# Second attention: one DMA transpose per query tile in place of two

## The chip, the cores and the metric

One of the eight cores of a Trainium2 chip runs the whole program. The metric is device time in microseconds (us), the median of some executions. Five engines work side by side, each in the order of its own instruction stream: TensorE (PE, its weight loads PEld), VectorE (DVE), ScalarE (ACT), GpSimd (POOL) and SyncE (SP), which here issues nearly all the DMAs. They meet only at semaphores.

## The reference

Two pre-norm layers over one sequence of 2048 tokens, width 256. Each layer adds an attention and a feed-forward block to the residual. The change touches the attention of the second layer alone:

```python
q = concat([q_c, rope(q_r)]); k = concat([k_c, rope(k_r)])   # 16 heads, 128 + 64 wide
scores = einsum('bqhd,bkhd->bhqk', q, k) / sqrt(128 + 64)     # no mask: 2048 x 2048 per head
probs  = softmax(scores)
ctx    = einsum('bhqk,bkhd->bqhd', probs, v)
x      = x + ctx @ out_w.T + out_b
```

## The kernel before

The second attention is worked off in 256 tiles: 16 heads by 16 tiles of 128 queries (`TILES = NH * NT`). The 2048 keys of a tile n come in two halves g = 0, 1 of 1024. All weights are folded so that keys and values share one 64-wide latent (`kv16`).

For each half: PE writes the scores into one of three score slots (`psS`, L1630 to L1632); DVE takes the row minimum of the negated scores (`half`, L1777 for half 0, L1782 for half 1, whose result is the shift of the whole tile); ACT takes the exponential into `prob` (`exponential`, L1968); ACT writes `prob`, lifted and rounded to fp16, as the high part (`high`, L1978); DVE writes the rest, again fp16, as the low part (`low`, L1790). Both parts of a half stand in `parts[:, s]`, 2 x 1024 columns in a ring of `RING = 4` halves, that is two tiles. Slot s is `(2n + g) % 4`. SP turns a slot by one DMA transpose into `partsT[:, s]`, sixteen blocks of 128 x 128 (`turn_probabilities`, L2164). PE then multiplies the turned blocks with the values (`context`, L1647 and L1648), 32 matmuls a half.

The order on each engine is written out by hand, one step per tile n:

- PE: scores (n+1, 0), scores (n+1, 1), a piece of the next head's projection in 12 of 16 tiles, context (n-2, 0), context (n-2, 1), the output projection of an older tile in every second head.
- DVE: half (n+1, 0), low (n, 0), half (n+1, 1), a rotation in 8 of 16 tiles (L1760), invert (n-2) (L1801), low (n, 1).
- ACT: exponential (n, 0), normalise (n-3), take_output, high (n, 0), exponential (n, 1), a rounding or folding in 8 of 16 tiles, high (n, 1).
- SP: transpose of (n, 0), once in four tiles of every second head the transpose of four tiles' contexts (`turn_contexts`, L2174, 8 blocks), transpose of (n, 1). Some weight loads of the feed-forward block stand between the tiles of the last two heads.
- POOL: small sums and splits, each placed behind a `low_done` count.

Two waits hang on the landing of a transpose. `high` (n, g) overwrites the slot of tile n-2 and waits until that slot's transpose has read it, that is, landed. `context` (n, g) waits for its own. The transpose of (n, g) itself waits for `low` (n, g), and for the context that last read its slot of `partsT` (`pv_done`). Each slot has a landing semaphore of its own. `turns(n, g)` counts how many times the slot of (n, g) has been used.

Of the kernel before, what the change touches and what calls it, by code (L numbers as in the profile page):

```python
# [44 lines left out]
def decoder_two_layers(nc, x_in, wq0, bq0, wk0, bk0, wv, bv, wout, bout, rwT, ewT, eb3, c_pick,  # L45
# [12 lines left out]
    pe, dve, act, pool, sp = nc.tensor, nc.vector, nc.scalar, nc.gpsimd, nc.sync  # L58
    top = ExitStack()

    def sb(ctx, name, shape, dt=F32, side=None):
        return ctx.enter_context(nc.sbuf_tensor(name, shape, dt, side=side))

    def sem(name):
        return top.enter_context(nc.semaphore(name))
# [1075 lines left out]
    def second_attention():  # L1141
# [314 lines left out]
        QS, RING = 5, 4  # L1456
# [7 lines left out]
        parts = sb(L, "parts", [P, RING, 2, HB], F16)  # L1464
        partsT = sb(L, "partsT", [P, RING, 2, HB // P, P], F16)
# [10 lines left out]
        folded, rested = sem("b_folded"), sem("b_rested")  # L1476
        score_ready, half_min, shift_ready, exp_done = sem("b_score"), sem("b_half_min"), sem("b_shift"), sem("b_exp")
        high_done, low_done = sem("b_high"), sem("b_low")
        landed = [sem(f"b_landed{s}") for s in range(RING)]
        pv_done, inverted, ctx_taken, ctx_split = sem("b_pv"), sem("b_inverted"), sem("b_ctx"), sem("b_ctx_split")  # L1480
        ctx_landed = [sem(f"b_ctx_landed{s}") for s in range(2)]
        out_ready, out_taken, out_added = sem("b_out"), sem("b_out_taken"), sem("b_out_added")
# [9 lines left out]
        TILES = NH * NT  # L1492
# [24 lines left out]
        def half_at(n, g):  # L1517

            return (2 * n + g) % RING

        def turns(n, g):

            return (2 * n + g) // RING + 1
# [15 lines left out]
        def outputs(n):  # L1539

            pairs, i = divmod(max(n, 0), 2 * NT)
            return pairs * NT + max(i - NT, 0)

        def has_output(n):
            return 0 <= n < TILES and n // NT % 2 == 1

        def batch(n):

            return (n // (2 * NT)) * (NT // BATCH) + n % NT // BATCH
# [33 lines left out]
        def tensor():  # L1583
# [51 lines left out]
            def context(n, g):  # L1635
                if not 0 <= n < TILES:
                    return
                s = half_at(n, g)
                pe.wait_ge(landed[s], 16 * turns(n, g))
                if g == 0 and n:  # L1640
                    pe.wait_ge(ctx_taken, n)
                taken = outputs(min(n + 2 - LATER, TILES - INTO_TAIL))
                if g == 0 and taken:
                    pe.wait_ge(out_taken, taken)
                for m in range(HB // P):
                    block = g * (HB // P) + m
                    pe.matmul(psO[:, 0:KW], partsT[:, s, 0, m, :], kv16[:, block, :], start=(block == 0), stop=False)  # L1647
                    ins = pe.matmul(psO[:, 0:REST], partsT[:, s, 1, m, :], kv16[:, block, 0:REST],  # L1648
                                    start=False, stop=(block == NT - 1))
                ins.then_inc(pv_done, 1)  # L1650
# [41 lines left out]
            for n in range(TILES + 2):  # L1692
                scores(n + 1, 0)
                scores(n + 1, 1)
                if n < TILES and piece_at(n) is not None:
                    project(n // NT + 1, piece_at(n))
                context(n - 2, 0)
                context(n - 2, 1)
                output(n - LATER)
                for i in units_at.get(n, ()):  # L1700
                    spread(i)
            for kind, *at in order:
# [15 lines left out]
                elif kind == "gate":  # L1718
                    c, m = at
# [212 lines left out]
        def scalar():  # L1932
# [38 lines left out]
            def high(n, g):  # L1971
                if n >= TILES:
                    return
                s = half_at(n, g)
                act.wait_ge(exp_done, 2 * n + g + 1)
                if turns(n, g) > 1:
                    act.wait_ge(landed[s], 16 * (turns(n, g) - 1))
                act.activation(parts[:, s, 0, :], prob[:, g, :], ACT.Copy, scale=LIFT).then_inc(high_done, 1)  # L1978

            def normalise(n):  # L1980
# [40 lines left out]
            for n in range(TILES + 3):  # L2021
                ahead = n < TILES and n // NT + 1 < NH
                exponential(n, 0)
                normalise(n - 3)
                take_output(n - LATER - 1)
                high(n, 0)
                exponential(n, 1)
                if ahead and n % NT in (3, 6, 9, 12):
                    round_queries(n // NT + 1, n % NT // 3 - 1, 2 * (n + 1))
                if ahead and n % NT in (4, 7, 10, 13):  # L2030
                    round_keys(n // NT + 1, n % NT // 3 - 1)
                if ahead and piece_at(n) is not None and piece_at(n) % 3 == 2:
                    fold(n // NT + 1, piece_at(n))
                high(n, 1)
                for i in units_at.get(n - 1, ()):
                    high_weights(i)
                if n == TILES + 1:
                    root(0)
            for kind, *at in order:
                if kind == "rows":  # L2040
                    g, = at
# [8 lines left out]
                elif kind == "gate":  # L2050
                    c, m = at
# [104 lines left out]
                butterfly(i)  # L2156

        def sync():
            def turn_probabilities(n, g):
                s = half_at(n, g)  # L2160
                sp.wait_ge(low_done, 2 * n + g + 1)
                if turns(n, g) > 1:
                    sp.wait_ge(pv_done, 2 * n + g + 1 - RING)
                sp.dma_start_transpose(partsT[:, s, :, :, :].rearrange("p a m q -> p (a m) q"),  # L2164
                                       parts[:, s, :, :].rearrange("p a k -> p (a k)")).then_inc(landed[s], 16)

            def turn_contexts(n):
                if not has_output(n) or n % BATCH != BATCH - 1:
                    return
                b, i = batch(n), n % NT - BATCH + 1  # L2170
                sp.wait_ge(ctx_split, 3 * (n + 1))
                if b >= 2:
                    sp.wait_ge(out_ready, BATCH * (b - 1))
                sp.dma_start_transpose(ctxT[:, b % 2, :, :],  # L2174
                                       ctxp[:, i:i + BATCH, :, :].rearrange("p t a c -> p (t a c)")).then_inc(ctx_landed[b % 2], 16)

            def load_small():
                sp.wait_ge(folded, 4 * NH)
                sp.dma_start(had[:, :, :], c_had.rearrange("s p n -> p s n")).then_inc(small_loaded, 16)
                sp.dma_start(su1[:, :], su_ug).then_inc(small_loaded, 16)  # L2180
                sp.dma_start(su2[:, :], su_dp).then_inc(small_loaded, 16)
                sp.dma_start(wsc[:, :, :], ws_ug).then_inc(small_loaded, 16)
                sp.dma_start(wsd[:, :], ws_dp.partition_broadcast(P)).then_inc(small_loaded, 16)

            loads_at = {TILES - 2 * NT + 3 * j + kind: (kind, j) for j in range(NB) for kind in range(2)}

            def load_up(kind, j):
                u, g, c = kind, j // 2, j % 2
                sp.wait_ge(rotated, 8 * (NH - 1) + 2 * j + kind + 1)
                rows = (wupT, wgateT)[u].rearrange("(k p) n -> p k n", p=P)  # L2190
                sp.dma_start(wug[:, u, g, c * BANK:(c + 1) * BANK], rows[:, g, c * BANK:(c + 1) * BANK]).then_inc(up_loaded, 16)

            def load_down():
                sp.wait_ge(score_ready, 2 * (TILES - NT))
                sp.dma_start(wdn[:, :, :], wdownT.rearrange("(k p) n -> p k n", p=P)).then_inc(down_loaded, 16)

            for n in range(TILES + 4):
                if n == TILES - NT - 3:
                    load_small()
                if n == TILES:  # L2200
                    load_down()
                if n - 2 in loads_at:
                    load_up(*loads_at[n - 2])
                if n < TILES:
                    turn_probabilities(n, 0)
                turn_contexts(n - 4)
                if n < TILES:
                    turn_probabilities(n, 1)
            for t in range(NT):
                sp.wait_ge(f_out_added, t + 1)  # L2210
                sp.dma_start(out[0, t * P:(t + 1) * P, :], ot[:, t % 2, :]).then_inc(stored[t % 2], 16)
            sp.wait_ge(stored[0], 16 * (NT // 2))
            sp.wait_ge(stored[1], 16 * (NT // 2))
# [3 lines left out]
        tensor()  # L2217
        gpsimd()
        sync()
        banks.close()  # L2220
        L.close()
        late.close()

    second_attention()
    top.close()

# [80 lines left out]
```

## Time and profile before

| | us |
|---|---|
| median of 3 runs | 2411.41 |
| lowest, highest | 2409.06, 2413.27 |
| the profiled execution's own time | 2413.38 |
| its span, first to last instruction | 2412.1 |

| engine | busy us | share of the span |
|---|---|---|
| PE | 2181.9 | 90% |
| PEld | 1589.3 | 66% |
| DVE | 2072.8 | 86% |
| ACT | 1832.1 | 76% |
| POOL | 1101.4 | 46% |

The span begins with the first layer; the second attention runs from about 780 us to 2230 us, the feed-forward block of the second layer behind it. In the rows further down, times are us from the start of the span, a row of a timeline gives start, duration, engine, line, operation and tiles, and in brackets the idle time before it with what ended that. The DMA share can exceed 1: it adds up the packets' own times on 16 engines, and these overlap.

### The profile page before, as it was taken

Reading aid. Unit: us, or ns where it says so; the run is one execution under the profiler, and the core shown is the slowest. Engines: PE = TensorE matmul, PEld = TensorE weight load, DVE = VectorE, ACT = ScalarE, POOL = GpSimd, SP = SyncE. Lnnn points to the kernel's source line nnn. Section 1 sums busy time; section 2 is a strip of 40 time slices with the busy share of each in tenths; the row PEclk is TensorE's granted clock in tenths of the full one; section 3 lists DMA queues with packets and bytes.
Section 4 is the critical chain, followed back from the end, with each engine's and each line's share of the span. In section 5 each row is a group of like instructions: output and inputs, shape, how many; then the busy total and the mean of one; then the engine's idle time right before and its main releaser. Section 6 shows DMA issues by size and latency. Waiting matters only on the chain.

```text
span 2412.1 us, 50636 instructions
## 1 busy us (share of the span) xinstructions
PE 2181.9 (90%) x18512; PEld 1589.3 (66%) x18512; DVE 2072.8 (86%) x3117; ACT 1832.1 (76%) x2622; POOL 1101.4 (46%) x1466
## 2 busy tenths in 40 slices
PE   4888888889987899999999999999999999889899
PEld 2444444456655677777777777777777777766687
DVE  6788888879987999999999999999999999887421
ACT  4877777756655889899898898888998988877411
POOL 3311211102224677657656666666756756622200
PEclk9999999989998999999999999999999999999899
DMA  3000000041000899999999999999999999999000
GB/s 132 1 1 2 2 1 2 1 96 38 5 1 1 148 196 198 198 198 196 197 195 195 195 200 195 197 194 199 198 196 198 195 199 195 200 193 202 9 18 18
DMA packets 1123542, 301.74 MB, mean 125 GB/s; under 512 B 1111456, under 2 KB 1120640, under 8 KB 1122432
## 3 DMA queue, kind: packets, MB, share of 16 engines
q1 hardware_dynamic: 1120448, 296.26, 71.1%
q8 instruction: 150, 2.46, 0.4%
q10 hardware_dynamic: 2848, 2.23, 0.3%
q14 instruction: 96, 0.79, 0.1%
HBM read 18.45 MB, written 2.10 MB: 9 GB/s over the span
## 4 chain that ended last, share of the span: by engine, by line
PE 22%; DVE 17%; DMA 11%; issue 10%; ACT 6%; POOL 1%; SPq 1%; DVEq 0%; ACTq 0%; POOLq 0%
DMA partsT<-parts 11%; DVE parts L1790 7%; DVE lows L1777 5%; DVE psS L1782 4%; PE psS L1727 4%; PE psOb L1647 3%; PE psS L1630 3%; ACT parts L1978 2%; ACT prob L1968 2%; PE psS L1632 2%; PE psS L1631 2%; PE psOb L1683 2%; PE psOb L1648 2%; DVE rot L1760 1%; PE psOb L1747 1%
## 5 line engine op out<-in xcount | busy, mean ns | idle before, releaser
L1790 DVE SCALAR_TENSOR_TENSOR parts<-prob,parts 128x1024 f16<-128x1024 f32 x512 | 677.4, 1323 | 37.0 <-ACT parts L1978 32.6
L1968 ACT ACTIVATE prob<-psS,shift 128x1024 f32<-128x1024 f32 x512 | 571.0, 1115 | 97.9 <-DVE psS L1782 90.2
L1978 ACT ACTIVATE parts<-prob 128x1024 f16<-128x1024 f32 x512 | 543.0, 1060 | 64.3 <-DMA partsT<-parts 59.3
L1630 PE MATMUL psS<-k_hi,q_lo 128*128 128x512 f32 x1024 | 446.4, 436 | 67.5 <-ACT prob L1968 56.8
L1647 PE MATMUL psOb<-kv,partsT 128*128 128x130 f16 x4096 | 401.6, 221 | 36.0 <-DMA partsT<-parts 35.6
L1647 PEld LDWEIGHTS psOb<-kv,partsT 128*128 128x128 f16 x4096 | 356.1, 97 | 113.7 <-issue 68.8
L1632 PE MATMUL psS<-k_hi,q_hi 128*128 128x512 f32 x1024 | 407.3, 398 | 0.0
L1631 PE MATMUL psS<-k_lo,q_hi 128*128 128x512 f32 x1024 | 405.7, 396 | 0.0
L1648 PE MATMUL psOb<-kv,partsT 128*128 128x66 f16 x4096 | 390.3, 192 | 0.0
L1648 PEld LDWEIGHTS psOb<-kv,partsT 128*128 128x128 f16 x4096 | 360.4, 98 | 1.0 <-issue 1.0
L1782 DVE TENSOR_SCALAR_CACHE_REDUCE psS<-psS,lows 128x1024 f32<-128x1024 f32 x256 | 328.5, 1283 | 1.8 <-PE psS L1632 1.8
L661 ACT ACTIVATE PT<-psS 128x1024 bf16<-128x1024 f32 (+1 forms) x320 | 278.4, 899 | 59.4 <-PE psS L410 35.9
L1777 DVE TENSOR_REDUCE lows<-psS 128x1 f32<-128x1024 f32 x256 | 311.1, 1215 | 5.8 <-PE psS L1632 4.2
L1630 PEld LDWEIGHTS psS<-k_hi,q_lo 128*128 128x128 f32 x1024 | 194.2, 190 | 170.8 <-ACT prob L1968 134.5
L2102 POOL TENSOR_TENSOR both_sums<-both_sums 128x64 f32<-128x64 f32 x256 | 170.7, 667 | 171.1 <-DVE parts L1790 143.1
L1632 PEld LDWEIGHTS psS<-k_hi,q_hi 128*128 128x128 f32 x1024 | 193.8, 189 | 46.2
L1631 PEld LDWEIGHTS psS<-k_lo,q_hi 128*128 128x128 f32 x1024 | 195.4, 191 | 26.0
L739 POOL TENSOR_TENSOR qB<-nmT,blocks 32x512 bf16<-32x512 bf16 x64 | 73.4, 1147 | 301.4 <-DVE qB L524 298.8
L410 PE MATMUL psS<-qB,kT 128*128 128x512 bf16 (+3 forms) x640 | 179.2, 351 | 12.1 <-ACT PT L661 12.0
L508 DVE TENSOR_REDUCE pm<-psT 128x1 f32<-128x512 f32 (+3 forms) x256 | 156.8, 613 | 37.4 <-PE psT L384 24.1
L508 DVE TENSOR_REDUCE pm<-psU 128x1 f32<-128x512 f32 (+2 forms) x255 | 150.2, 589 | 22.6 <-PE psU L384 11.5
L2072 POOL TENSOR_TENSOR whole<-rot 64x512 f32<-64x512 f32 x64 | 82.7, 1293 | 129.1 <-DVE parts L1790 122.5
(294 smaller groups left out, 4091.4 us busy)
## 6 DMA issues: line engine op xcount, KB each, us to landing
partsT<-parts SPq DMA_TRANSPOSE x512, 4.9
ef<-in_ewT SPq DMA_DIRECT2D x1, 2048.0 KB, 10.3
rf<-in_rwT SPq DMA_DIRECT2D x1, 2048.0 KB, 10.3
outw_s<-in_outwT SPq DMA_DIRECT2D x1, 2048.0 KB, 9.5
trig<-in_trig SPq DMA_DIRECT2D x2, 1024.0 KB, 10.6
out_x<-ot SPq DMA_DIRECT2D x16, 128.0 KB, 1.7
wug<-in_wupT SPq DMA_DIRECT2D x4, 256.0 KB, 3.6
wug<-in_wgateT SPq DMA_DIRECT2D x4, 256.0 KB, 3.8
```

The source lines that it names most:

```text
L508: dve.tensor_reduce(pm[:, h, r, j:j + 1], max_banks[max_place[n["max"]]][:, 0:w], AX_X, ALU.max).then_inc(max_taken, 1)
L661: act.activation(PT[:, h, first:first + width], psS[:, x * BANK:x * BANK + width], ACT.Exp).then_inc(exp_done, 1)
L1630: pe.matmul(bank, q_lo[:, slot, q], k_hi[b][:, k], start=True, stop=False)
L1631: pe.matmul(bank, q_hi[:, slot, q], k_lo[b][:, k], start=False, stop=False)
L1632: ins = pe.matmul(bank, q_hi[:, slot, q], k_hi[b][:, k], start=False, stop=True)
L1647: pe.matmul(psO[:, 0:KW], partsT[:, s, 0, m, :], kv16[:, block, :], start=(block == 0), stop=False)
L1648: ins = pe.matmul(psO[:, 0:REST], partsT[:, s, 1, m, :], kv16[:, block, 0:REST], start=False, stop=(block == NT - 1))
L1777: dve.tensor_reduce(lows[:, n % 2:n % 2 + 1], here, AX_X, ALU.min).then_inc(half_min, 1)
L1782: dve.tensor_scalar(here, here, 0.0, lows[:, n % 2:n % 2 + 1], ALU.add, ALU.min, accum_out=shift[:, n % 2:n % 2 + 1]).then_inc(shift_ready, 1)
L1790: dve.scalar_tensor_tensor(out=parts[:, s, 1, :], in0=prob[:, g, :], scalar=LIFT, in1=parts[:, s, 0, :], op0=ALU.mult, op1=ALU.subtract).t ...
L1968: act.activation(prob[:, g, :], psS[:, (2 * n + g) % 3, :], ACT.Exp, bias=shift[:, n % 2:n % 2 + 1], scale=-1.0).then_inc(exp_done, 1)
L1978: act.activation(parts[:, s, 0, :], prob[:, g, :], ACT.Copy, scale=LIFT).then_inc(high_done, 1)
```

## The change

The probabilities' transposes of a tile's two halves become one: SP waits for the second `low` of the tile and issues one transpose of `parts[:, s:s+2]`, 32 blocks of 128 x 128, into `partsT[:, s:s+2]`. It waits for the context of the second half of tile n-2, not the first. There are two landing semaphores, one for each pair of slots. `high` and `context` wait on them in half 0 only; half 1 follows on the same engine. The transpose of the contexts now stands behind the tile's one transpose.

```diff
-        landed = [sem(f"b_landed{s}") for s in range(RING)]
+        landed = [sem(f"b_landed{s}") for s in range(RING // 2)]
...
             def context(n, g):
...
-                pe.wait_ge(landed[s], 16 * turns(n, g))
+                if g == 0:
+                    pe.wait_ge(landed[s // 2], 16 * turns(n, g))
...
             def high(n, g):
...
-                if turns(n, g) > 1:
-                    act.wait_ge(landed[s], 16 * (turns(n, g) - 1))
+                if g == 0 and turns(n, g) > 1:
+                    act.wait_ge(landed[s // 2], 16 * (turns(n, g) - 1))
...
-            def turn_probabilities(n, g):
-                s = half_at(n, g)
-                sp.wait_ge(low_done, 2 * n + g + 1)
-                if turns(n, g) > 1:
-                    sp.wait_ge(pv_done, 2 * n + g + 1 - RING)
-                sp.dma_start_transpose(partsT[:, s, :, :, :].rearrange("p a m q -> p (a m) q"),
-                                       parts[:, s, :, :].rearrange("p a k -> p (a k)")).then_inc(landed[s], 16)
+            def turn_probabilities(n):
+                s = half_at(n, 0)
+                sp.wait_ge(low_done, 2 * n + 2)
+                if turns(n, 0) > 1:
+                    sp.wait_ge(pv_done, 2 * n + 2 - RING)
+                sp.dma_start_transpose(partsT[:, s:s + 2, :, :, :].rearrange("p g a m q -> p (g a m) q"),
+                                       parts[:, s:s + 2, :, :].rearrange("p g a k -> p (g a k)")).then_inc(landed[s // 2], 16)
...
                 if n < TILES:
-                    turn_probabilities(n, 0)
+                    turn_probabilities(n)
                 turn_contexts(n - 4)
-                if n < TILES:
-                    turn_probabilities(n, 1)
```

## Rows read from the trace of the kernel before

**Rows 1.** Windows: busy us of each engine, clock, DMA share, GB/s.

```profile
core 0: us, PE busy (x) PEld busy (x) DVE busy (x) ACT busy (x) POOL busy (x), PEclk, DMA share, GB/s
1400.00:1600.00 200.00, 188.47 (x1748) 148.45 (x1748) 192.74 (x239) 178.28 (x223) 125.67 (x184) 1.00 1.17 197
2110.00:2160.00 50.00, 39.72 (x361) 30.41 (x359) 42.10 (x51) 37.81 (x45) 11.47 (x29) 0.97 1.10 192
```

**Rows 2.** Transposes of L2164 in 1000:2000, then in 2000:2240.

```profile
L2164 SPq DMA_TRANSPOSE partsT<-parts x363: 1323/2449/4172, 999.5 to 1999.5; - x182
...
DMA to landing us min/median/max: 4.3/5.0/7.1
...
L2164 SPq DMA_TRANSPOSE partsT<-parts x77: 1395/2492/4375, 1999.5 to 2224.0; - x77
```

**Rows 3.** Waits in 1000:2000: who waited for whom, us, times, longest.

```profile
ACT prob L1968 <- DVE psS L1782: 59.2, 88, 1.3
...
ACT parts L1978 <- DMA partsT<-parts: 31.8, 36, 2.0
...
PE psOb L1647 <- DMA partsT<-parts: 16.9, 24, 1.5
DVE parts L1790 <- ACT parts L1978: 15.3, 31, 1.4
```

**Rows 4.** Timeline of SP, two stretches: how transposes are issued.

```profile
795.66 4.31 SPq L2164 DMA_TRANSPOSE partsT<-parts  x2
...
1501.56 1.85 SPq L2174 DMA_TRANSPOSE ctxT<-ctxp  x1
1503.50 15.61 SPq L2164 DMA_TRANSPOSE partsT<-parts  x6
```

**Rows 5.** Timeline of DVE: the second step without a rotation.

```profile
1593.10 1.21 DVE L1790 SCALAR_TENSOR_TENSOR parts<-prob,parts 128x1024 f16<-128x1024 f32 x1
1594.22 1.22 DVE L1777 TENSOR_REDUCE lows<-psS 128x1 f32<-128x1024 f32 x1
1595.35 1.22 DVE L1790 SCALAR_TENSOR_TENSOR parts<-prob,parts 128x1024 f16<-128x1024 f32 x1
1596.48 1.29 DVE L1782 TENSOR_SCALAR_CACHE_REDUCE psS<-psS,lows 128x1024 f32<-128x1024 f32 x1
...
1603.22 1.25 DVE L1790 SCALAR_TENSOR_TENSOR parts<-prob,parts 128x1024 f16<-128x1024 f32 x1
```

**Rows 6.** Timeline of ACT beside it.

```profile
1602.13 1.06 ACT L1978 ACTIVATE parts<-prob 128x1024 f16<-128x1024 f32 x1
...
1604.48 1.06 ACT L1978 ACTIVATE parts<-prob 128x1024 f16<-128x1024 f32 x1
1605.42 1.12 ACT L1968 ACTIVATE prob<-psS,shift 128x1024 f32<-128x1024 f32 x1
```

**Rows 7.** Transposes of 8 blocks: hS alone in its stretch, then ctxT.

```profile
L761 SPq DMA_TRANSPOSE hS<-hB x4: 1232/1248/1339, 495.8 to 604.3; - x4
...
DMA to landing us min/median/max: 3.1/3.1/4.2
...
L2174 SPq DMA_TRANSPOSE ctxT<-ctxp x32: 1232/1464/1948, 923.6 to 2235.5; - x32
...
DMA to landing us min/median/max: 3.1/3.8/5.8
```

**Rows 8.** Windows: before, within and behind a lone transpose; queued; a stall; behind it.

```profile
795.70:796.70 1.00, 1.00 (x6) 0.82 (x5) 1.00 (x1) 0.70 (x1) 0.00 (x0) 1.00 0.00 0
797.00:799.00 2.00, 1.12 (x5) 0.77 (x5) 2.00 (x3) 1.97 (x2) 0.20 (x1) 1.00 1.16 214
1518.50:1522.50 4.00, 4.00 (x48) 3.37 (x47) 4.00 (x5) 2.81 (x5) 2.56 (x5) 1.00 1.15 213
1496.25:1497.25 1.00, 1.00 (x10) 0.88 (x7) 1.00 (x4) 0.54 (x2) 0.84 (x3) 1.00 0.04 4
1497.50:1499.50 2.00, 1.81 (x9) 1.15 (x8) 1.98 (x2) 1.82 (x4) 1.37 (x2) 1.00 1.18 266
```

**Rows 9.** DMA queues in 1495:1498, then 1000:2000: packets, MB, share.

```profile
GB/s 225 208 212 215 218 188 215 212 222 212 215 403 222 133 68 14 7 0 0 0 0 0 0 0 3 7 10 7 10 10 10 7 10 10 10 188 280 300 290 280
...
q8 instruction: 1, 0.02, 2.1%
...
q1 hardware_dynamic: 775422, 195.42, 115.7%
q8 instruction: 70, 1.15, 0.4%
```

**Rows 10.** Timeline of PE: one half's scores, then both contexts up to the next scores.

```profile
1604.38 0.50 PE L1630 MATMUL psS<-k_hi,q_lo 128*128 128x512 f32 x1
...
1605.88 0.40 PE L1598 MATMUL psPb<-lat_hi,wr_lo 128*128 128x512 f32 x1
...
1606.59 0.23 PE L1647 MATMUL psOb<-kv,partsT 128*128 128x130 f16 x1
...
1607.99 0.48 PE L1630 MATMUL psS<-k_hi,q_lo 128*128 128x512 f32 x1
```

## The prediction

> **What bounds the kernel now.** I read the windows of the second attention first. Between 1400 and 1600 us DVE is busy 192.74 of 200 us, PE 188.47, ACT 178.28, and the DMA engines move 197 GB/s [rows 1]. So DVE leads, and three others are close. The count of transposes gives the pace: 363 in 1000 us are 181.5 tiles, 5.51 us a tile [rows 2]. DVE's own work in a tile is then 5.51 x 192.74 / 200 = 5.31 us. The waits come next. In 1000 us `high` on ACT waits 31.8 us for a landing, PE's `context` 16.9 us, DVE's `low` 15.3 us for `high` [rows 3]. The landings cost about 0.1 to 0.2 us a tile now.
>
> SP's timeline says how full the queue of transposes is. Six issues from 1503.50 take 15.61 us without a gap, 2.6 us each [rows 4], and a median issue lasts 2.449 us [rows 2]: two of them are 4.9 to 5.2 us of a 5.51 us tile. So the queue is nearly full, DVE is nearly full, and neither can be called the only bound. The change relieves the queue a little and lengthens the way from `low` to landing. The question is which of the two decides.
>
> **What the change removes.** One issue per tile, 256 in all. Queued transposes are 2.6 us apart, but their data alone is 0.524 MB, which at the 213 GB/s of the queued stretch [rows 8] take 2.46 us. So an issue costs the queue some 0.15 us beyond its data. All of it on the path would be 256 x 0.15 = 38 us; it is worth nothing when the queue is no longer the bound. DVE's 5.31 us is the floor of a tile, so no relief of the queue can give more than (5.51 - 5.31) x 256 = 51 us. The waits dropped from half 1 on PE and ACT cost nothing then and now: an already fulfilled wait stands in front of work that takes 1.06 us and more [rows 6]. Between 0 and 0.05 us for each, and I take 0.
>
> **What the change moves.** The first half of tile n used to be sent off behind `low` (n, 0). Now it goes behind `low` (n, 1), and both halves land together. `high` (n, 0) waits for the landing of tile n-2. That closes a loop of two tiles: end of `low` (n-2, 1), issue, landing, `high` (n, 0), `low` (n, 0), `half` (n+1, 1), rotation, invert, `low` (n, 1). The time of a tile can't be under half of this loop. In the kernel before, each half had a loop of its own, with only one `high` and one `low` in it (2.3 us beside the flight), and that left room.
>
> *The part on the engines.* From `high` to `low`: `high` at 1602.13, its `low` at 1603.22, 1.09 us [rows 5, 6]. From `low` (n, 0) to the end of `low` (n, 1) DVE does everything of a tile but the first minimum, which takes from 1594.22 to 1595.35, 1.13 us [rows 5]: 5.31 - 1.13 = 4.18 us. This average has the rotations and the stretched `low`s in it. Together 5.27 us. ACT's branch is shorter: `high` 0.94, exponential 1.1, `high` 1.06 and `low` 1.2 are 4.3 us, 4.95 with a fold or rounding in between, so DVE decides. I add 0.05 us each for semaphore to issue and landing to ACT: 5.37 us.
>
> *The flight.* No transpose of 32 blocks is in the trace. Of 8 blocks there are four that had the queue to themselves, 3.1 us each, and the shortest of 16 blocks takes 4.3 us [rows 2, 7]. So 8 more blocks cost 1.2 us, which agrees with the windows: nothing moves in the first us behind an issue, then 214 GB/s, lone or queued [rows 8]. Sixteen blocks more are 2.4 us: 4.3 + 2.4 = 6.7 us. It can hardly be less unless the rate changes; for a low end I take the 266 GB/s seen behind a stall [rows 8], 1.05 MB / 266 = 3.95 us plus the 1.85 us that are not data (4.3 - 2.46), 5.8 us. For the high end the median landing of today with its queueing, 5.0 us [rows 2], and a whole further issue of 2.6 us: 7.6 us. I take 6.7 and no queueing: one issue of some 4.9 us stands in a tile of 6.2 us.
>
> *The stalls.* A window of 1 us shows 4 GB/s, with 266 GB/s behind it [rows 8]; cut finer (40 slices of 3 us) the hole is 1.5 us long [rows 9]. In these 3 us one 16 KB packet of an instruction queue passes, and there are 70 of those in 1000 us, 0.39 a tile [rows 9]. I take it that each such packet holds the transposes up for some 1.25 to 1.5 us. What was held up is made good at 266 against 213 GB/s, so a hole early in a transpose costs next to nothing and one at its end 1 to 1.2 us; say 0.6. The flow fills some 80% of the time: 0.39 x 0.8 x 0.6 = 0.2 us. With a little for ctxT meeting the next transpose (32 times 1.2 us) I take a flight of 7.0 us.
>
> The loop is 7.0 + 5.37 = 12.37 us, 6.19 us a tile, 0.68 over today's 5.51. By the bounds: 5.8 gives 5.59, 7.6 plus 0.2 gives 6.6.
>
> *What else waits on the later landing.* PE's `context` (n-2) starts at the landing and both halves take 1.4 us [rows 10]. The scores of tile n+2 need exponential (n, 1), 2.1 us behind the landing (`high` 0.94, exponential 1.1, rows 6), and last 1.5 us a half [rows 10]; DVE wants them when `low` (n, 1) is through, 5.3 us behind it. So PE stays ahead by more than 1 us, though it idles 15% instead of 6%. The transpose of n waits for `pv_done` of n-2, which comes 1.5 us behind the landing, the transpose 5.3. SP has behind the waiting transpose only ctxT, whose readers run five tiles late, and late loads. POOL follows DVE's count and has slack. None adds.
>
> **The sum.** Up to 2000 us, 218 tiles run at 5.51. 218 x 0.68 = 148 us. From 1999.5 to 2224.0 there are 77 transposes, 38.5 tiles at 5.83 us [rows 2]: loads share the queue and the clock is at its lower level (1.2 GHz) for short pieces, 0.97 over a window [rows 1]. Part of this hides in the loop's slack; 38 x 0.43 = 16 us. The end of the attention comes 2 us later, the longer flight of the last tile. Together 166 us on the profiled execution's 2413.4: 2579. The median of the runs is 2 us under that execution: 2577.
>
> **Rival A, not slower.** The flow of a bigger transpose is quicker and the saved issues come through. It lives in the flight: a tile takes the larger of 5.31 and (flight + 5.37) / 2, so it decides when the flight is under 5.65 us. At 5.8 the time is 2411 + 256 x 0.08, 2431; at 5.2 or less the tile falls to DVE's 5.31, 51 us gained, 2360. For it speaks that the engines did move 266 GB/s; against it, that they did so only behind a stall, and that lone transposes of 8 and 16 blocks both go at the slow rate. A flight of 4.4 us, if it existed, would be this case in full.
>
> The Trainium skill is on this side ("DMA: Bandwidth & Descriptors", Anatomy of one DMA): a fixed 2.0 us and 436 GB/s, measured on GpSimd's path, would be an estimated 4.4 us for this transfer, and its Bandwidth section wants batches of 1 MiB or more. This case's trace disagrees in the slope, 214 GB/s against 436, and agrees in the fixed part, 1.85 us. The same page (Latency and other measured facts) gives transposes 261 GB/s, by an estimate 5.9 us here, 5.6 us a tile.
>
> **Rival B, PE.** With 85% in place of 94% busy, PE's clock may be at 1.2 GHz more often. In 2110:2160 it was busy 39.72 of 50 us at a mean of 0.97 [rows 1]: 3% of PE's time, 1.5 us in 50. If this held all along, up to 0.2 us a tile: 50 us on top, 2627. Against it: a PE that stays 1 us ahead swallows most.
>
> **Rival C, the neighbours meet.** The loops of even and odd tiles are independent, and can drift until a tile follows its neighbour by DVE's 5.3 us, little over one transpose. Then each hole or ctxT delays two flights. The flight is 7.8 us, the tile 6.6: 256 x 1.07 = 274, 2685.
>
> **Numbers.** Forecast 0.73, rival A 0.12, B 0.09, C 0.06. 2577 is the forecast's. Its own range goes from a flight of 6.4 us (5.89 a tile, +98, 2510) to 7.4 us (6.39, +220, 2633). To leave out no more than 2 in 10 I reach into B, and a bit toward A: 2495 to 2645. Under 0.2% (5 us) no change can be told. Faster 0.08 (two thirds of A), same 0.02, slower 0.90.
>
> **What would show it.** In the changed profile: transposes half as many, landing at a minimum near 6.7 and a median near 7 us; `high` waiting for the DMA some 0.5 us and more in most tiles, well over 100 us in 1000; DVE busy near 5.3 / 6.2 = 86% in the windows; GB/s near 176. SP's queue with gaps. The prediction is wrong if the median landing is under 6 us, if DVE stays over 94% busy, or if ACT's wait for the landing remains at 30 us while the pace falls: then something other than this loop sets it.

## The result

| | before | after |
|---|---|---|
| median, us | 2412.34 | 2637.43 |
| lowest to highest, us | 2409.06 to 2414.01 | 2634.82 to 2639.51 |

The ratio is 1.0937, 95% interval [1.0923, 1.0951]: 225 us slower. The forecast was 166 us slower, 2577 us, with a range from 2495 to 2645. The measured time lies near the range's upper end, 60 us above the forecast.

The profile after, engine by engine:

```profile
span 2633.5 us, 49784 instructions
...
PE 2217.1 (84%) x18424; PEld 1583.6 (60%) x18512; DVE 2071.3 (79%) x3117; ACT 1849.2 (70%) x2622; POOL 1057.1 (40%) x1466
```

DVE does the same 2071 us of work as before (2072.8); its share fell because the span grew. The window that answers to [rows 1], with DVE at 82% in place of 96%, and 168 GB/s in place of 197:

```profile
1400.00:1600.00 200.00, 168.05 (x1510) 127.71 (x1508) 164.42 (x201) 154.31 (x191) 103.83 (x145) 1.00 0.94 168
```

The transposes in 1000:2000 (count, shortest/median/longest issue in ns, first and last start), and their flights, for [rows 2]:

```profile
L2165 SPq DMA_TRANSPOSE partsT<-parts x155: 4677/4877/6420, 999.7 to 1996.7; - x155
...
DMA to landing us min/median/max: 6.6/6.8/9.3
```

154 steps from 999.7 to 1996.7 are 6.47 us a tile, against 5.51. The waits of the same stretch, for [rows 3]:

```profile
PEld psS L1630 <- ACT prob L1969: 205.2, 208, 1.7
ACT parts L1979 <- DMA partsT<-parts: 183.5, 118, 3.7
DVE parts L1791 <- ACT parts L1979: 175.6, 147, 3.5
...
ACT prob L1969 <- DVE psS L1783: 30.0, 55, 1.2
```

`high` now waits 183.5 us for the landing (31.8 before), and DVE's `low` waits 175.6 us for `high` (15.3 before). The chain that ended last says the same: it spends 45% of the span in the flight of the transpose, where it spent 11%. The chain by line before, then by engine and by line after:

```profile
DMA partsT<-parts 11%; DVE parts L1790 7%; DVE lows L1777 5%; DVE psS L1782 4%; PE psS L1727 4%; PE psOb L1647 3%; PE psS L1630 3%; ACT parts L1978 2%; ACT prob L1968 2%; PE psS L1632 2%; PE psS L1631 2%; PE psOb L1683 2%; PE psOb L1648 2%; DVE rot L1760 1%; PE psOb L1747 1%
...
DMA 46%; PE 11%; DVE 6%; issue 4%; ACT 4%; SPq 0%; DVEq 0%; POOL 0%; ACTq 0%
DMA partsT<-parts 45%; PE psS L1728 3%; DVE psS L1783 3%; ACT parts L1979 2%; DVE parts L1791 1%; PE psOb L1648 1%; ACT prob L1969 1%; PE psOb L1748 1%; PE psPb L1748 1%; PE psOb L1684 1%; PE psS L1630 1%; PE psOb L1649 1%; PE psS L1631 0%; PE psS L1632 0%; PE psS L1663 0%
```

The loop itself can be read off two timelines. DVE first: the second `low`s of two tiles, and the first `low` of the tile behind them.

```profile
1030.90 2.09 DVE L1791 SCALAR_TENSOR_TENSOR parts<-prob,parts 128x1024 f16<-128x1024 f32 x1
...
1037.67 1.20 DVE L1791 SCALAR_TENSOR_TENSOR parts<-prob,parts 128x1024 f16<-128x1024 f32 x1
...
1040.85 1.23 DVE L1791 SCALAR_TENSOR_TENSOR parts<-prob,parts 128x1024 f16<-128x1024 f32 x1 [0.84 <-ACT parts L1979]
```

And ACT, the two `high`s of half 0 that wait for these tiles' landings:

```profile
1039.76 1.06 ACT L1979 ACTIVATE parts<-prob 128x1024 f16<-128x1024 f32 x1 [0.91 <-DMA partsT<-parts]
...
1047.27 1.06 ACT L1979 ACTIVATE parts<-prob 128x1024 f16<-128x1024 f32 x1 [2.16 <-DMA partsT<-parts]
```

The second `low` that ends at 1032.99 lets the `high` two tiles further on go at 1039.76, 6.8 us later: a flight that nothing delayed. The one that ends at 1038.87 lets it go at 1047.27, 8.4 us later. What lies between is in two windows, and in the queues of 1043.5:1048.5:

```profile
1044.00:1045.00 1.00, 0.46 (x2) 0.42 (x3) 1.00 (x2) 1.00 (x3) 0.94 (x2) 1.00 1.15 223
1045.00:1046.00 1.00, 1.00 (x6) 0.81 (x5) 1.00 (x2) 0.11 (x1) 0.84 (x3) 1.00 0.04 5
...
q8 instruction: 1, 0.02, 1.1%
```

A hole (223 GB/s, then 5 GB/s) begins some 6 us behind the issue, when most of the data are through, and one 16 KB instruction packet passes in these 5 us, as in [rows 9].

### The profile page after: what moved, and what is told of

It is laid out like the page before. It is cut to its first block, busy times and chain, and to the rows that moved or that the text cites. A ratio compares the mean times of both kernels' runs of the same rounds, so it can differ in the third digit from the quotient of the medians.

```text
span 2633.5 us, 49784 instructions
## 1 busy us (share of the span) xinstructions
PE 2217.1 (84%) x18424; PEld 1583.6 (60%) x18512; DVE 2071.3 (79%) x3117; ACT 1849.2 (70%) x2622; POOL 1057.1 (40%) x1466
## 4 chain that ended last, share of the span: by engine, by line
DMA 46%; PE 11%; DVE 6%; issue 4%; ACT 4%; SPq 0%; DVEq 0%; POOL 0%; ACTq 0%
DMA partsT<-parts 45%; PE psS L1728 3%; DVE psS L1783 3%; ACT parts L1979 2%; DVE parts L1791 1%; PE psOb L1648 1%; ACT prob L1969 1%; PE psOb L1748 1%; PE psPb L1748 1%; PE psOb L1684 1%; PE psS L1630 1%; PE psOb L1649 1%; PE psS L1631 0%; PE psS L1632 0%; PE psS L1663 0%
## 5 line engine op out<-in xcount | busy, mean ns | idle before, releaser
L1630 PE MATMUL psS<-k_hi,q_lo 128*128 128x512 f32 x1024 | 456.4, 446 | 233.7 <-ACT prob L1969 224.4
L1648 PE MATMUL psOb<-kv,partsT 128*128 128x130 f16 x4096 | 394.5, 221 | 45.4 <-DMA partsT<-parts 44.8
L1649 PE MATMUL psOb<-kv,partsT 128*128 128x66 f16 x4096 | 385.0, 193 | 0.0
L410 PE MATMUL psS<-qB,kT 128*128 128x512 bf16 (+3 forms) x600 | 168.0, 346 | 17.4 <-ACT PT L661 15.2
```

Source lines behind the costliest of these rows:

```text
L1630: pe.matmul(bank, q_lo[:, slot, q], k_hi[b][:, k], start=True, stop=False)
```

## The experiments

All times are medians; the kernel before stood at 2410 to 2412 us in the same rounds. The changed kernel was timed in the first round alone, so differences against its 2637 us carry the 2 us or so between rounds. "Over tiles" means an average over the timeline rows of the tiles between 850 and 2000 us, 160 to 210 of them by the kernel's pace. A loop's flight is counted from SP's issue to the start of `high` two tiles on, its engine part from that start to the next issue; half their sum is the tile's time in any kernel with a ring of two tiles, whether or not the loop binds. What shows that it binds is that the waits stand in it.

**e1: both transposes behind the second `low`.** In the kernel before:

```diff
-                sp.wait_ge(low_done, 2 * n + g + 1)
+                sp.wait_ge(low_done, 2 * n + 2)
```

> The kernel before, except that SP sends the two transposes of a tile one behind the other when the second low is through: as late as in the changed kernel, but in two pieces with a landing each. Loop theory (the tile is half of flight + engine part, and high of half 0 waits for the whole flight): the first piece lands 4.4 us behind its issue in place of 6.8, the loop of half 0 is (4.4 + 0.6 for holes + 5.5) / 2 = 5.25 us and no longer binds; the time is that of the queue and DVE, 2405 to 2440 us. Rival 'lateness' (what costs is that nothing is sent before the second low): as slow as the changed kernel, 2600 or more.

2475.77 us, ratio 1.0269 [1.025, 1.0288]. Neither of the two: 64 us, above the loop theory's 2440 and far from 225. The flights are short again, and `high` waits 84.7 us in place of 183.5:

```profile
L2164 SPq DMA_TRANSPOSE partsT<-parts x343: 1317/2308/4351, 998.3 to 1998.8; - x172
...
  ACT parts L1978: 84.7, 95
  PEld psOb L1647: 60.8, 71
...
DMA to landing us min/median/max: 4.2/4.8/6.8
...
DVE parts L1790 <- ACT parts L1978: 42.1, 62, 1.8
...
DVE rden L1801 <- PE psOb L1648: 24.1, 20, 2.9
```

The late sending alone costs a quarter of what was lost. The second half waits for the first in the queue, 3.0 us from the end of its `low` to its issue over tiles, and then lands 4.8 us later (median); PE's `context`, which needs it, waits 60.8 us. The miss has two parts. The loop of half 0, which was forecast not to bind, still does in some tiles: half of `high`'s wait (43.5 of 84.7 us) is in half 0, and DVE's `low` waits 42.1 us for `high` (15.3 in the kernel before). And DVE's invert waits 24.1 us for the late `context` (12.4 before).

**e2: sent early, awaited together.** In the kernel before, `high` and `context` of half 0 wait for both landings of the tile:

```diff
-                pe.wait_ge(landed[s], 16 * turns(n, g))
+                if g == 0:
+                    for h in range(2):
+                        pe.wait_ge(landed[s + h], 16 * turns(n, g))
```

(The same on ACT for `high`, with turns less one.)

> The kernel before, with both transposes sent as early as before, but high and context of half 0 wait for the landings of both halves of the tile. Loop theory: the second half's flight is that of a 16-block transpose behind its low, 4.9 us and 0.4 for holes, the loop (5.3 + 5.5) / 2 = 5.4 us, about as long as a tile now takes; 2415 to 2470 us. Rival 'lateness': 2405 to 2420, since the issues are as early as before. Rival 'joint landing': that both halves must have landed is what costs, then most of the 225 us come back, 2550 or more.

2444.30 us, ratio 1.0147 [1.0131, 1.0162]: within the loop theory's 2415 to 2470, and outside both rivals' ranges. Over tiles, 5.4 us pass from the issue of the second half to `high` (n, 0), as forecast (5.3), and a tile takes 5.69 us. The engine part came out at 6.0 us, not 5.5, since the second half's issue follows its `low` by 0.5 us, with SP still busy with the first. All of `high`'s wait is now in half 0:

```profile
DVE parts L1792 <- ACT parts L1981: 59.6, 84, 2.1
ACT parts L1981 <- DMA partsT<-parts: 58.2, 69, 2.0
```

Late sending alone costs 64 us, the joint wait alone 34. Together in one transpose they cost 225, more than the sum. That fits a loop that each alone leaves near the length of DVE's tile, and that only both together make much longer.

**e3 and e7: what stands in the loop.** In the changed kernel DVE's rotation goes behind the second `low`, with the invert (e3) or without (e7):

```diff
...
-                    rotate(n // NT + 1, piece_at(n))
-                invert(n - 2)                       # e3 only
...
                 low(n, 1)
...
+                    rotate(n // NT + 1, piece_at(n))
+                invert(n - 2)                       # e3 only
```

> The changed kernel with the rotation and the invert on DVE placed behind the second low of the tile instead of before it. The same instructions on every engine. Loop theory: 0.66 us leave the loop in 8 of 16 tiles and 0.1 in all, less where ACT's branch then decides; about 0.3 us of a loop of two tiles, 0.15 a tile, 2637 - 38 = 2600 us (2585 to 2615). If DVE's total work or the queue were the bound: no change, 2637.

2655.23 us, ratio 1.1018 [1.1002, 1.1035]: 18 us slower than the changed kernel, where 38 were to be gained. The way from `low` 0 to `low` 1 did shrink, from 2.88 to 2.52 us over tiles. But ACT's `normalise`, which stands in front of `high`, now waits for the invert:

```profile
ACT both_sums L1988 <- DVE rden L1802: 121.8, 135, 1.3
...
ACT parts L1979 <- DMA partsT<-parts: 70.5, 64, 3.5
```

So the forecast of e3 failed by a second loop that the edit opened. e7 leaves the invert where it was:

> The changed kernel with the rotation alone behind the second low; the invert stays in front of it. In e3 ACT's normalise of tile n-3, which stands before high (n, 0), waited 121.8 us in 1000 for the invert behind the second low: a new loop of one tile, 1.1 + 2.5 + 1.2 + 0.66 + 0.16 + 0.84 = 6.46 us. Without it the loop theory gets its gain after all: some 0.3 us shorter from low 0 to low 1 in a loop of two tiles, 0.14 a tile, 2637 - 36 = 2600 us (2590 to 2615). Rival (a later rotation delays PE's projection and that is what e3 paid for): 2640 to 2660 again.

2629.58 us, ratio 1.0901 [1.0884, 1.0918]: 8 us faster than the changed kernel, not 36, and outside the 2590 to 2615. The sign is the loop theory's, the size isn't, and the rival (2640 to 2660) is out. `low` 0 to `low` 1 is 2.58 us over tiles (2.88), but `high` to `low` is 1.20 (1.14) and the second `low` takes 1.46 (1.37), so the engine part only falls from 5.48 to 5.33 us, and the flight came out 0.07 us longer. Half of (0.15 - 0.07) a tile is 10 us. Why `high` to `low` and the second `low` got longer, no run shows.

**e4 and e5: a third tile in the ring.** The parts get a third pair of slots; the turned parts stay at two tiles. e4 is the changed kernel with it, e5 the one before. The room comes from one rest of weights (`qr_lo`), which both leave out.

```diff
-        qr_lo = [sb(L, f"qr_lo{r}", [P, NH, C], F32R) for r in range(2)]
+        qr_lo, third = qr_hi, sb(L, "third", [P, 2, 2, 2 * BANK], F16)
...
-                if g == 0 and turns(n, g) > 1:
-                    act.wait_ge(landed[s // 2], 16 * (turns(n, g) - 1))
+                if g == 0 and n >= 3:
+                    act.wait_ge(landed[half_at(n - 3, 0) // 2], 16 * turns(n - 3, 0))
```

> The changed kernel with a third pair of slots for the parts before the transpose (the turned parts keep their ring of two tiles), so high of tile n waits for the landing of tile n-3. The 8 KB for it are taken from the rests of 32 KB of rotary weights, which are left out: the rounded weights stand in their place in the products, with the same instructions in the attention. Loop theory: the loop spans three tiles, (7.45 + 5.5) / 3 = 4.3 us, and no longer binds; DVE's 5.31 us and the queue's 5.0 + holes give 5.35 to 5.55 a tile, 2360 to 2420 us, perhaps below the kernel before. Rival 'the bigger transpose is slow in itself' (the queue moves less): stays above 2550.

2473.97 us, ratio 1.0274 [1.0257, 1.0292]. It gives back 163 of the 225 us, with transposes as big as in the changed kernel. The median flight is still 7.0 us. So it was `high`'s wait, and neither the size nor the rate of the transposes, that cost most. But it isn't the 2360 to 2420 forecast: PE's `context` now waits longest for the landing, and DVE's invert for PE.

```profile
PEld psOb L1650 <- DMA partsT<-parts: 82.0, 66, 3.3
DVE rden L1803 <- PE psOb L1651: 62.1, 48, 3.6
...
PEld psOb L1650 <- DMA partsT<-third: 43.1, 33, 3.2
```

e5, the control:

> The kernel before with the third pair of slots of e4 (the same rests of weights left out), one transpose a half. If the waits of high for a landing are what DVE loses in the kernel before (31.8 us in 1000), 20 to 40 us are gained, 2370 to 2390. If the queue (5.0 us a tile and the holes) is the bound of the kernel before, nothing: 2405 to 2415. Beside e4 it gives the cost of one transpose per tile where high doesn't wait for it: 60 to 100 us by PE's context, which still waits.

2407.48 us, ratio 0.9985 [0.9976, 0.9995]: 4 us. In the kernel before, freeing `high` is worth next to nothing; its 31.8 us of waits in 1000 were slack. DVE stays busy for 191.06 of 200 us in 1400:1600, so DVE or the queue keeps the pace; this run doesn't tell which. Beside e4 it prices one transpose per tile where `high` is free of it: 66 us, within the 60 to 100 expected.

**e6, e9, e10: PE's share.** PE's 16 matmuls a tile on the turned low parts are left out of the computation: of the changed kernel (e6), of e4 (e9) and of e5 (e10).

```diff
...
-                    ins = pe.matmul(psO[:, 0:REST], partsT[:, s, 1, m, :], kv16[:, block, 0:REST],
-                                    start=False, stop=(block == NT - 1))
...
```

First e6:

> The changed kernel without the 16 matmuls a tile that multiply the turned low parts with the values (left out of the computation). PE has some 28 in place of 44 matmuls a tile and its context takes 0.7 in place of 1.4 us. Loop theory: PE isn't in the loop; fewer instruction fetches (0.39 a tile to 0.25) spare the flight some 0.2 us, 0.1 a tile: 2637 - 26 = 2611 us (2600 to 2630). Rival 'PE decides' (context behind the landing, or its 84% busy): 0.7 us a tile, or half of it in a loop of two tiles, 2460 to 2550.

2599.97 us, ratio 1.0787 [1.0767, 1.0808], at the lower edge of the loop theory's 2600 to 2630, 37 us under the changed kernel; the rival's 2460 to 2550 is out. PE's `context` is half as long, PE is busy 158.93 of 200 us in 1400:1600 in place of 168.05, and the tile hardly cares. The 16 KB fetches in 1000 us, after and then e6:

```profile
q8 instruction: 60, 0.98, 0.4%
...
q8 instruction: 41, 0.67, 0.3%
```

Over tiles, issue to `high` is 7.23 us in place of 7.45, and the tile 0.10 us shorter: about half of 0.22. The traced execution took 2607 us, so these rows explain some 25 of the median's 37 us.

Then e9:

> e4 (changed kernel, third pair of slots) without the 16 matmuls a tile for the low parts of the values, as e6 has it. Theory: with high free of the landing, a second loop of two tiles goes through PE: landing, context, invert, second low, issue; 7.3 + 1.4 + 0.3 + 1.3 = 10.3 us and what PE has in front of the context. The context shorter by 0.7 us gives 0.35 us a tile, with fewer holes some 0.4: 2474 - 100 = 2375 to 2410. If the rest of e4 is the holes alone: 2474 - 26 = 2448.

2423.59 us, ratio 1.0053 [1.0036, 1.0069], 50 us under e4, less than forecast, and outside its 2375 to 2410.

And its control, e10:

> The control of e9: e5 (kernel before, third pair of slots) without the same matmuls. No loop through a landing binds here; DVE's 5.31 us a tile stays, the queue has fewer holes: 2407 - 20 = 2380 to 2400.

2384.84 us, ratio 0.9894 [0.988, 0.9909], 23 us under e5, as forecast. So 23 of e9's 50 us are what the control shows as well, and the other 27 need the transpose per tile; that they belong to PE's way behind the landing is argued from the waits of e4, not isolated. What is left between e9 and e10, 39 us, no run takes apart.

**e11: a longer flight.** In the changed kernel SP sends an idle transpose of 4 blocks in front of each tile's:

```diff
+                if n:
+                    sp.wait_ge(idled, 16 * n)
+                sp.dma_start_transpose(idle[:, :, :], kv16[:, :, :].rearrange("p b c -> p (b c)")[:, 0:4 * P]).then_inc(idled, 16)
```

> The changed kernel with an idle DMA transpose of 4 blocks (nobody reads it) in front of each tile's transpose. It lengthens the way from the second low to the landing by a delay d that the trace will show: at least 0.75 us (0.6 for its data at 214 GB/s, 0.15 an issue), up to 1.4 if SP holds its next issue back as it does behind the 8-block transposes (1.23 us). The queue then works 6.2 us of a tile of 7, so it isn't the bound. Loop theory: half of d a tile, 254 x d / 2 on top of 2637: 2732 at 0.75, 2815 at 1.4. If the queue's total work were the bound of the changed kernel: the full d a tile, 2830 to 2990. If the flight weren't in the bound: 2640 to 2660.

2804.62 us, ratio 1.1635 [1.1616, 1.1654]: 167 us on top. SP's timeline gives d:

```profile
1500.96 1.19 SPq L2169 DMA_TRANSPOSE idle<-kv  x1
1502.20 4.97 SPq L2170 DMA_TRANSPOSE partsT<-parts  x1
```

1.24 us here, 1.29 over tiles. 254 x 1.29 / 2 = 164 us. Half the delay a tile is what a loop of two tiles pays; a full queue would have paid all of it, 328 us. The close agreement is helped by two small differences that cancel in part: the idle transpose itself starts 0.3 us behind the second `low` where the tile's started 0.08 behind it, and the flight to `high` was 0.16 us shorter (7.29). With both, the loop grows by 1.35 us and the tile by 0.68, from 6.47 to 7.15.

**e8: the rotation in the kernel before.** As e7, in the kernel without the change.

> The kernel before with the rotation behind the second low of the tile. Where no loop of two tiles through the landing binds, the place of the rotation changes nothing: 2405 to 2415. If sending the second half 0.66 us earlier in half of the tiles fills the queue better, up to 15 us less.

2413.92 us, ratio 1.001 [1.0, 1.0019]. The place of the rotation is indifferent there.

## Why the prediction was right, and what was mis-sized

**The mechanism stands.** The forecast named a loop of two tiles, (flight + engine part) / 2. Two runs hold to it closely: 1.29 us more ahead of the landing gave 167 us where half a delay a tile makes 164 (e11), and 0.22 us less in the flight gave 0.10 us a tile (e6). One shows which wait it is: the same big transposes without the wait of `high` gave back 163 us (e4). A weak fourth has the right sign alone: the rotation's place matters only where the loop binds (8 us gained in e7 where 36 were forecast, none in e8).

**The flight without delays was right**: 6.7 us forecast from 8 and 16 blocks. Over tiles, 38 of 178 flights had no instruction packet from 1 us before the issue to the landing and no ctxT beside them. They landed after 6.70 us on average and reached `high` in 6.79 (forecast 6.75). Rival A, the quicker big transpose, is out, and with it the estimates of 4.4 and 5.9 us: the flow is 218 GB/s or so here too:

```profile
1036.00:1038.00 2.00, 1.58 (x8) 0.97 (x6) 2.00 (x5) 1.91 (x3) 1.63 (x2) 1.00 1.17 218
```

**The term that was too small is "the stalls".** I gave 0.2 us for the holes and 0.1 for ctxT, a flight of 7.0, 7.05 to `high`. It is 7.45 over tiles, so the delays are worth 0.66 us and not 0.3: that is 0.36 of the 0.40 us missing. There were as many 16 KB packets a tile as forecast (60 in 155 tiles, 0.39), and ctxT cost next to nothing (11 flights with it alone: 6.87 us to `high`). What was wrong is the price of a packet. I had let the holes fall anywhere in the flight, at 0.6 us each. They don't:

| packets between issue and landing | flights | to landing, us | to `high`, us |
|---|---|---|---|
| none, no ctxT | 38 | 6.70 | 6.79 |
| 16 KB, 4.5 us or more behind the issue | 50 | 8.14 | 8.22 |
| 16 KB, in the first 2.5 us, none late | 35 | 6.99 | 7.52 |
| no 16 KB; 8 KB, 4.5 us or more behind the issue | 16 | 7.21 | 7.35 |

The late 16 KB packets alone add 0.40 us to the average flight. A late hole can't be made good, since hardly any data are left to catch up with. An early one is nearly made good by the landing; `high` then still comes 0.5 us behind it. In 22 of these 35 the flight before had a late packet, each time the same one, since flights of 7.3 us at 6.47 us a tile overlap. So that tile ran late, which is the likely reason; it adds 0.14 us. The last row names packets that I had overlooked altogether, on a second instruction queue:

```profile
q14 instruction: 47, 0.39, 0.1%
...
q14 instruction: 36, 0.29, 0.1%
```

(the kernel before, then after, 1000:2000). That the holes cluster at the end has a likely reason that no run isolates: the fetches follow PE's progress, PE resumes at a landing, and the loop gives landing and next flight a fixed distance. Two runs fit. e6, where PE has fewer instructions, has 18 flights with a late 16 KB packet in place of 50. e11, where the distance is another, has 18 too, with nearly as many packets (62 in place of 69).

**The engine part was 0.16 us short**: 5.37 forecast with 0.05 for the landing, so 5.32, and 5.48 over tiles: 1.14 `high` to `low`, 2.88 to the second `low`, 1.46 from its start to the issue. I had taken DVE's mean busy time; the mean of the larger of DVE's and ACT's branch may be more, e.g. in the tiles with a fold on ACT. No run separates the two.

Together (0.40 + 0.16) / 2 = 0.28 us a tile, 6.19 to 6.47, and 218 x 0.28 = 61 us: the whole miss of 59. The last 37 tiles went from 5.94 to 6.44 us, 18 us where 16 were forecast.

**Luck in the range.** The forecast's own range ended at a flight of 7.4 us and 2633 us. The measured 7.45 us and 2637 us lie just outside it. That 2637 is inside the stated range is owed to the reach up to 2645, which was made for rival B, a cause that didn't come.

**The other rivals.** B, PE and its clock: the windows of 200 us from 1000 to 2400 show a granted clock of 0.98 to 1.00 with PE 81 to 86% busy, the two extremes here:

```profile
1800.00:2000.00 200.00, 171.02 (x1524) 131.28 (x1522) 166.80 (x204) 156.66 (x195) 106.95 (x155) 0.98 0.94 168
...
2200.00:2400.00 200.00, 161.60 (x1478) 121.67 (x1477) 160.85 (x195) 151.82 (x186) 84.35 (x138) 1.00 1.00 180
```

Over the whole span it was granted 0.986 (0.982 before), so nothing was added by it. C, neighbours that meet: issues were 4.8 to 9.4 us apart. Ten of the 178 followed their neighbour within 5.1 us, and only one of them had no packet. One hole often touches two flights, as C says, but the second still lands after 6.99 us, far from C's 7.8. It isn't the main cause.

**What the change was worth in itself.** One issue fewer per tile relieved a queue that wasn't the only bound. SP's median issue fell from 2 x 2.449 to 4.877 us, which is nothing. The supposed 0.15 us an issue is not visible in the result, and no run isolates it.

**A slip in the text.** "None adds" was true of the changed kernel only as long as `high`'s wait was longer. e4 shows a second way of two tiles right behind it: landing, `context`, invert, second `low`, issue. DVE's invert waits 62.1 us there for PE. But over tiles this way leaves about 1.0 of its 11.6 us idle between its steps, and is without a gap in 40 of 198 tiles. So it explains part of e4's 5.8 us a tile, and what sets the rest stays open.

## What to carry to other kernels

Where a buffer ring closes a loop through a DMA, write the loop down: (flight + work in the loop) / ring depth. Merging two transfers adds the second one's data to the flight and makes the first piece wait for the last producer; in this kernel that would have been free only with a loop shorter than the busiest engine's tile, and one forecast at 5.25 us, just under DVE's 5.31, still bound in part of the tiles (e1). Before moving work out of such a loop, look for the waits of one tile's distance that it opens (e3), and before deepening the ring, for the next way that the landing delays, here over the other buffer (e4). And where something can stop a transfer, ask when in the transfer it comes: an average price for a hole was the term that failed here.

## What the runs showed of the hardware

- The DMA transpose from SBUF to SBUF flowed at 213 to 218 GB/s for 16 and for 32 blocks of 128 x 128 fp16. The shortest flights of 4, 8, 16 and 32 blocks were 2.4, 3.1, 4.3 and 6.6 us, 0.6 to 0.7 us for each 4 blocks behind the first 4.
- A 16 KB instruction packet goes with a hole in such a transpose. Averaged over the 81 of them in 850:2000 of the kernel before, the flow is under 50 GB/s from 0.5 to 1.75 us behind the packet's start, and then 257 to 284 GB/s for some 2 us. The 8 KB packets of the second instruction queue (54 there) show a shorter one, 64 to 79 GB/s for half a microsecond. A hole costs little early in a transfer (landing after 7.0 us) and nearly its full length at the end: 8.1 us in place of 6.7.
- SP holds a 32-block issue for 4.9 us, as long as two 16-block ones at their median of 2.45. The shortest were 4.7 and 1.3 us. Merging saved no issue time here.
